# Queries and keys split into rounded and remaining parts before the turn instead of after it

## The reference, cut to what matters

```python
h = concatenate([patch_sums(x) @ channel_weights, txt], axis=1)      # 64 x 228 x 192
xn = norm_scale * layernorm(h) + norm_bias
q, k, v = split(xn @ W_attn + b_attn)                                # 12 heads x 16
q, k = rope(q), rope(k)                                              # rotation by position
att = softmax([sinks, causal(q @ k.T / 4)])[..., 1:]
h = h + ((att @ v) @ W_proj + b_proj) * rezero
h = h + experts(layernorm(h))          # 8 experts, top 2, capacity, gated by silu
```

## Time and profile before

| | us |
|---|---|
| median of 3 executions | 3388.71 (3383.93 to 3389.58) |
| profiled execution, span of its instructions (no other time of it is given) | 3385.4 |
| DVE busy over the span | 2468.5 (73%) |
| PE busy over the span | 3004.5 (89%) |
| POOL busy over the span | 2034.5 (60%) |
| ACT busy over the span | 1363.1 (40%) |

### The profile page before, as it was taken

How to read it: one execution, slowest core, us unless ns; L and a number is a source line. 1 busy time by engine, 2 the same in 40 slices (tenths; PEclk the granted TensorE clock), 3 DMA queues, 4 the chain that set the end, 5 groups by cost and what they waited for, 6 DMA issues and landing times.

```text
span 3385.4 us, 62750 instructions
## 1 busy us (share of the span) xinstructions
PE 3004.5 (89%) x20432; PEld 2601.3 (77%) x20432; DVE 2468.5 (73%) x6258; ACT 1363.1 (40%) x3398; POOL 2034.5 (60%) x1558
## 2 busy tenths in 40 slices
PE   2988889888889888898898898599999999999997
PEld 1777767777777777777777777598989898898987
DVE  3899998999998999989989987354444444444553
ACT  0434444344344344343443444343344443443443
POOL 2666666666666666666666664255555555555655
PEclk9899998999998999989988989799999999999999
DMA  6544544433333333233233320233333333433333
GB/s 190 150 131 138 155 126 138 130 85 102 90 89 103 82 97 103 77 101 99 80 101 89 90 75 23 68 51 62 52 67 49 66 57 56 69 50 65 51 62 48
DMA packets 205961, 297.49 MB, mean 88 GB/s; under 512 B 88374, under 2 KB 167675, under 8 KB 205874
## 3 DMA queue, kind: packets, MB, share of 16 engines
q1 hardware_dynamic: 82994, 243.82, 26.1%
q0 software_dynamic: 122880, 52.55, 11.1%
HBM read 201.73 MB, written 93.90 MB: 87 GB/s over the span
## 4 chain that ended last, share of the span: by engine, by line
issue 31%; POOL 27%; DVE 20%; DMA 12%; PE 7%; POOLq 1%; SPq 1%; ACT 1%; DVEq 0%; ACTq 0%
DMA out<-arena,who 10%; POOL out L1437 8%; POOL moe_rows L1268 6%; POOL qk L721 4%; POOL arena L689 4%; DVE hot L631 3%; DVE place L669 3%; POOL rstd L707 3%; POOL spread L697 3%; DVE arena L1419 2%; DVE pooled L498 2%; DVE pieces L550 2%; PE bank L1409 2%; DVE rot_s L535 1%; DMA prob<-in_w_t 1%
## 5 line engine op out<-in xcount | busy, mean ns | idle before, releaser
L1437 POOL DMA_INDIRECT out<-arena,who x320 | 597.2, 1866 | 202.9 <-issue 198.7
L721 POOL TENSOR_TENSOR qk<-rot_c,rot_s 114x768 f32<-114x768 f32 x256 | 455.2, 1801 | 256.7 <-DVE rot_s L535 253.6
L1395 ACT ACTIVATE arena<-bank 128x456 f32<-128x456 f32 x320 | 175.5, 549 | 634.2 <-PE bank L1386 621.8
L1409 PE MATMUL bank<-prob,arena 128*114 128x192 f32 x2560 | 429.3, 326 | 0.0
L689 POOL TENSOR_TENSOR arena<-arena 112x896 f32<-112x896 f32 x192 | 396.8, 2096 | 44.3 <-DMA arena<-in_x 44.3
L1409 PEld LDWEIGHTS bank<-prob,arena 128*114 128x114 f32 x2560 | 412.2, 178 | 0.0
L1268 POOL DMA_INDIRECT moe_rows<-row,slot x256 | 293.1, 1145 | 185.3 <-issue 185.3
L1401 DVE TENSOR_TENSOR arena<-bank,arena 128x456 f32<-128x456 f32 x320 | 201.7, 630 | 268.5 <-ACT arena L1395 256.6
L571 DVE TENSOR_REDUCE top<-bank 114x2 f32<-114x456 f32 (+1 forms) x576 | 332.0, 622 | 2.5 <-PE bank L903 2.0
L843 PE MATMUL bank<-w_qkv,xn_t 97*114 97x384 f32 x512 | 221.3, 561 | 109.4 <-DVE place L669 108.7
L1426 POOL TENSOR_TENSOR rms<-rms,minus_half 114x4 f32<-114x4 f32 x82 | 85.4, 1042 | 348.0 <-DVE rms L1324 348.0
(11 more groups left out here) (167 smaller groups left out, 7523.2 us busy)
## 6 DMA issues: line engine op xcount, KB each, us to landing
arena<-in_x SPq DMA_DIRECT2D x64, 2352.0 KB, 11.3
arena<-moe_rows SPq DMA_DIRECT2D x82, 363.4 KB
moe_rows<-filler SPq DMA_DIRECT2D x20, 1453.5 KB
out<-h SPq DMA_DIRECT2D x64, 171.0 KB
out<-arena,who POOLq DMA_INDIRECT x320
arena<-in_w_t SPq DMA_DIRECT2D x9, 512.0 KB
arena<-in_w_t SPq DMA_DIRECT2D x18, 256.0 KB
moe_rows<-row,slot POOLq DMA_INDIRECT x256
```

What stands on the lines that cost most here:

```text
L721: nc.gpsimd.tensor_tensor(dst, a, b, ALU.add).then_inc(qk_rotated[t], 1)
L1409: ins = nc.tensor.matmul(bank[6 + s // 2][0:TT, D * (s % 2):D * (s % 2 + 1)], hid[:, j, TT * s:TT * (s + 1)], w_dn[e_par][:, j, :], start= ...
L1437: nc.gpsimd.indirect_dma_start(out=out[:, :], out_offset=bass.IndirectOffsetOnAxis(ap=who[par][:, s:s + 1], axis=0), in_=ys[par][:, s, :], ...
```

## The change

Rounding and subtraction are done while the tokens still lie on the partitions. POOL adds the rotation once, in place in `rot_c` (two instructions of 192 columns for a half). ACT (`high_parts`) then copies the sum into the two rounded places of each head in `qk`, which is now an fp32r tile, in two instructions of 384 columns for a half. POOL (`low_parts`) subtracts what ACT wrote from the sum and writes the two remaining places, again two instructions of 384 columns. The turn becomes a plain matmul with the rounded identity, and what comes out is only copied: a turn of queries by ACT (`place_q`, two instructions), a turn of keys by DVE (`place_k`, one). `round_qk`, `split_qk` and `rounded` are gone.

```diff
-        qk = sb("qk", [TT, 2, 2 * HEADS, 4, HD])
+        qk = sb("qk", [TT, 2, 2 * HEADS, 4, HD], fp32r)
...
         def rotate(dve, at, t):
...
-            wait(dve, qk_rotated[t], 2 * at.b)
+            wait(dve, qk_low[t], at.b)
...
+        def place_q(act, at, r):
+            act.wait_ge(qk_turned[r], at.b + 1)
+            if r == 0:
+                wait(act, scored_t[8], at.b - 1)
...
+                ins = nc.scalar.activation(dst, src[lo, 0:4 * TT].rearrange("p (a n) -> p a n", a=2), ACT.Copy)
+            ins.then_inc(qk_placed[r], 1)
+        def place_k(dve, at, r):
+            dve.wait_ge(qk_turned[r], at.b + 1)
...
+            nc.vector.tensor_copy(dst, src).then_inc(qk_placed[r], 1)
...
         def add_rotation(pool, at, t):
+            pool.wait_ge(qk_read[t], at.b + 1)
             for half in range(2):
-                nc.gpsimd.tensor_tensor(dst, a, b, ALU.add).then_inc(qk_rotated[t], 1)
+                c, sn = (r[:, t, :].rearrange("p (a s k) -> p a s k", s=2, k=8)[:, :, i, :]
+                         for r, i in ((rot_c, half), (rot_s, 1 - half)))
+                ins = nc.gpsimd.tensor_tensor(c, c, sn, ALU.add)
+            ins.then_inc(qk_rotated[t], 1)
+        def low_parts(pool, at, t):
+            pool.wait_ge(qk_high[t], at.b + 1)
+            for hi, lo, of, first in piece_views(t):
+                ins = nc.gpsimd.tensor_tensor(lo, of, first.bitcast(fp32), ALU.subtract)
+            ins.then_inc(qk_low[t], 1)
...
+        def high_parts(act, at, t):
+            act.wait_ge(qk_rotated[t], at.b + 1)
+            wait(act, qk_turned[5], at.b)
+            for hi, lo, of, first in piece_views(t):
+                ins = nc.scalar.activation(hi, of, ACT.Copy)
+            ins.then_inc(qk_high[t], 1)
...
         def turn_qk(pe, at, last, r):
-                pe.wait_ge(qk_rotated[1], 2 * n)
-                pe.wait_ge(qk_rotated[0], 2 * n)
+                pe.wait_ge(qk_low[1], n)
+                pe.wait_ge(qk_low[0], n)
...
-                    ins = nc.tensor.transpose(dst[:, TT * (2 * a + t):TT * (2 * a + t + 1)], src, ident[0:TT, 0:TT])
+                    ins = nc.tensor.matmul(dst[:, TT * (2 * a + t):TT * (2 * a + t + 1)], src, ident_r[0:TT, 0:TT],
+                                           start=True, stop=True)
...
         def step_scalar(act, p, a, m, t, z):
             half1("T5 S7 S8")
+            if a:
+                high_parts(act, a, 0)
             if t:
                 copy_y(act, t)
+            if a:
+                high_parts(act, a, 1)
             if t:
                 copy_yn(act, t)
...
         def step_vector(dve, p, a, m, t, z):
             # split_qk 0, 2, 4 are gone; 1, 3, 5 are place_k at the same places
...
                 if a:
                     add_rotation(pool, a, 0)
+                    low_parts(pool, a, 0)
                 if z:
                     scatter_waits(pool, z, fill)
                 if a:
                     add_rotation(pool, a, 1)
+                    low_parts(pool, a, 1)
```

More of the change, by code:

```diff
@@ L198, in build @@
         rot_s = sb("rot_s", [TT, 2, 2 * D])
-        qk = sb("qk", [TT, 2, 2 * HEADS, 4, HD])
+        qk = sb("qk", [TT, 2, 2 * HEADS, 4, HD], fp32r)
         val = [sb(f"val{i}", [TT + 1, 2, HEADS, 32]) for i in range(2)]
-        rounded = [sb(f"rounded{i}", [128, 4 * TT], fp32r) for i in range(2)]
         pieces = sb("pieces", [128, 16 * HID + 4 * ROWS], fp32r)
@@ L309, in build @@
         qk_rotated = [sem(f"qk_rotated{t}") for t in range(2)]
+        qk_high = [sem(f"qk_high{t}") for t in range(2)]
+        qk_low = [sem(f"qk_low{t}") for t in range(2)]
         qk_turned = [sem(f"qk_turned{k}") for k in range(6)]
-        qk_rounded = sem("qk_rounded")
-        qk_split = [sem(f"qk_split{k}") for k in range(6)]
+        qk_placed = [sem(f"qk_placed{k}") for k in range(6)]
         scored = [sem(f"scored{k}") for k in range(9)]
@@ L536, in rotate @@
                                     sin[:, t, :].unsqueeze(1).to_broadcast([TT, 24, 16]), ALU.mult).then_inc(qk_read[t], 1)
-        def split_qk(dve, at, r):
-            dve.wait_ge(qk_rounded, 6 * at.b + r + 1)
-            src, hi = bank[bank_of("turn", r)], rounded[r % 2]
+        def place_q(act, at, r):
+            act.wait_ge(qk_turned[r], at.b + 1)
+            if r == 0:
+                wait(act, scored_t[8], at.b - 1)
             k = TURNS[r]
-            if r == 0:
-                wait(dve, scored_t[8], at.b - 1)
[L545 to L559, removed]
@@ new lines, in place_q @@
+            src = bank[bank_of("turn", r)]
+            for side in range(2):
+                lo = slice(64 * side, 64 * side + 64)
+                dst = q_t[at.par][lo, :, :].rearrange("p (a s) n -> p a s n", s=2)[:, 2 * k:2 * k + 2, side, :]
+                ins = nc.scalar.activation(dst, src[lo, 0:4 * TT].rearrange("p (a n) -> p a n", a=2), ACT.Copy)
+            ins.then_inc(qk_placed[r], 1)
+        def place_k(dve, at, r):
+            dve.wait_ge(qk_turned[r], at.b + 1)
+            if r == 1:
+                wait(dve, scored_t[8], at.b - 1)
+            kk = TURNS[r] - 3
+            dst = k_t[at.par][:, 2 * kk:2 * kk + 2, :, 0:TT].rearrange("p a t n -> p (a t) n")
+            src = bank[bank_of("turn", r)][:, 0:4 * TT].rearrange("p (a n) -> p a n", a=4)
+            nc.vector.tensor_copy(dst, src).then_inc(qk_placed[r], 1)
@@ L711, in add_rotation, with piece_views @@
         def add_rotation(pool, at, t):
[L712 to L715, removed]
+            pool.wait_ge(qk_read[t], at.b + 1)
             for half in range(2):
[L717 to L720, removed]
-                nc.gpsimd.tensor_tensor(dst, a, b, ALU.add).then_inc(qk_rotated[t], 1)
+                c, sn = (r[:, t, :].rearrange("p (a s k) -> p a s k", s=2, k=8)[:, :, i, :]
[7 more added lines that the diff above has]
+            ins.then_inc(qk_low[t], 1)
+        def piece_views(t):
+            for side in range(2):
+                heads = slice(HEADS * side, HEADS * (side + 1))
+                of = rot_c[:, t, D * side:D * (side + 1)].rearrange("p (a k) -> p a k", k=HD)
+                of, first = (v.unsqueeze(2).to_broadcast([TT, HEADS, 2, HD]) for v in (of, qk[:, t, heads, 0, :]))
+                if side == 0:
+                    parts = qk[:, t, heads, :, :].rearrange("p a (c s) k -> p a s c k", s=2)
+                else:
+                    parts = qk[:, t, heads, :, :].rearrange("p a (s c) k -> p a s c k", s=2)
+                yield parts[:, :, 0, :, :], parts[:, :, 1, :, :], of, first
+        def high_parts(act, at, t):
[4 more added lines that the diff above has]
+            ins.then_inc(qk_high[t], 1)
         def copy_h(act, at):
@@ L764, in copy_v @@
                                  bank[6][0:TT, 0:2 * D].rearrange("p (a k) -> p a k", k=HD), ACT.Copy).then_inc(v_ready, 1)
[L766 to L773, removed]
         def round_shift(act, at):
@@ L866, in bank_free @@
                 if kind == "turn" and m:
-                    return pe.wait_ge(qk_split[k], m.b + 1)
+                    return pe.wait_ge(qk_placed[k], m.b + 1)
                 if kind == "score" and m:
@@ L894, in score @@
             if k < 3:
-                pe.wait_ge(qk_split[2 * k], n)
-                pe.wait_ge(qk_split[2 * k + 1], n)
+                pe.wait_ge(qk_placed[2 * k], n)
+                pe.wait_ge(qk_placed[2 * k + 1], n)
             bank_free(pe, "score", k, at, last)
@@ L1093, in half1 @@
                 for c, k in items.split():
-                    if c == "T" and m:
-                        round_qk(act, m, int(k))
+                    if c == "T" and m and TURNS[int(k)] < 3:
+                        place_q(act, m, int(k))
                     elif c == "S" and t:
@@ L1130, in step_vector @@
         def step_vector(dve, p, a, m, t, z):
-            if m:
-                split_qk(dve, m, 0)
             if t:
@@ L1137, in step_vector @@
             if m:
-                split_qk(dve, m, 1)
+                place_k(dve, m, 1)
             if a:
@@ L1141, in step_vector @@
             if m:
-                split_qk(dve, m, 2)
-            if m:
-                split_qk(dve, m, 3)
+                place_k(dve, m, 3)
             if p:
@@ L1148, in step_vector @@
                 choose(dve, z)
-            if m:
-                split_qk(dve, m, 4)
             if z:
@@ L1157, in step_vector @@
             if m:
-                split_qk(dve, m, 5)
+                place_k(dve, m, 5)
             if p:
```

## The result

The changed kernel takes 3520.7 us (median of 4, 3515.8 to 3528.3) against 3389.1: ratio 1.0394, 95% interval 1.0377 to 1.0410. Forecast were 3485, slower, from 3325 to 3530.

What follows compares the result with a forecast made beforehand. DVE's list was taken to bound pass one at 32.09 us a step. Afterwards a POOL, ACT, PE chain of 31.3 plus 2.4 of clock cost makes 33.7, +96 us on 3388.7: 3485 us, range 3325 to 3530.

Steps and rivals of the forecast that it cites:

- The bound moves from DVE to the chain of hand-overs: Pass one: the chain POOL, ACT, PE sets the step instead of DVE, 31.3 us at full clock against 32.09.
- The pause before `project`: PE has nothing to do from 23.3 to 27.7 us of each step, 4.4 us, as `copy_yn` stands behind `high_parts` 1.
- The clock's price: Half clock on PE's work behind the pause, `project` to `sum_channels`: 2.4 us a step, of between 0 and 3.5.
- Rival 1: PE's pause doesn't bring the clock down, or only under the pause: step 31.3 us, 3341 us in all; chance 0.22.
- The last exponential: On ACT it was to start 15.46 us after `sum_channels`, kept as in the kernel before.
- The turn at nothing: PE's 24 transposes become 24 matmuls of fp32r pieces: priced nothing to 0.6 us a step, nothing taken.
- L669 and those behind it: DVE's stand at L669 and the next instruction, behind POOL's: from up to 1.8 to about 0.5 us each.
- POOL's price by columns: POOL at 2.2 ns a column: 0.52 us for 192 columns (adds), 0.95 for 384 (low parts).
- the gap ahead of the first scatter: On POOL, from low part to first scatter DMA: 0.3 to 1.05 us, 0.6 taken.
- Rival 4: New operations are dearer: 3690 us by POOL's low parts, 3620 by two-record turns, 3515 in milder forms; chance 0.09.
- The range's upper end: 3530 us, from 3.0 us of clock cost a step and the late scatter gap.
- Rival 3: Hand-overs hidden, the step falls with DVE's work until PE bounds it at 29 us: 3203 us; chance 0.04.

Runs made afterwards that it cites:

- e6_before_order: Kernel before, with POOL's list reordered (rotation of half 1 and `spread` ahead of the scatters): 3396.9 us, ratio 1.0028.
- e1_fill: Changed kernel with 17 throw-away matmuls in PE's list ahead of `project`: 3387.3 us, ratio 0.9996.
- e8_fill_transpose: Changed kernel with 17 throw-away matmuls ahead of `project` and the turns as transposes again: 3355.8 us, ratio 0.9911.
- e11_fill_gap: Changed kernel with 17 throw-away matmuls ahead of `project` and `exp_gap` moved behind S5 on ACT: 3358.6 us, ratio 0.9907.
- e2_transpose: Changed kernel with the turns made as transposes again: 3516.6 us, ratio 1.0381.
- e12_order_gap: Changed kernel with scatters last on POOL, turns as transposes, five throw-away matmuls ahead of `turn_xf`, `exp_gap` behind turn 4: 3112.9 us, ratio 0.9186.
- e4_gap: Changed kernel with `exp_gap` moved behind turn 4 and S5 in ACT's list: 3639.6 us, ratio 1.0747.
- e9_before_fill: Kernel before, with eight throw-away matmuls ahead of the second `make_qk`: 3379.7 us, ratio 0.9984.

## Why the prediction was right

The forecast held by its mechanism, not only by its sign: the pause, its cause, the clock behind it and its price came as forecast. Part of the closeness is luck, as errors along the chain cancel. In us from `sum_channels`, for the step shown (1022.88) and as the mean of the 59 steps:

| step | forecast | step shown | mean |
|---|---|---|---|
| last exponential starts | 15.46 | 16.65 | 16.26 |
| low parts 0 done | 18.9 | 20.1 | 19.7 |
| first scatter | 19.5 | 20.3 | 19.9 |
| adds 1 done | 26.0 | 26.9 | 26.5 |
| last score done | 23.3 | 24.6 | 24.2 |
| `project` | 27.7 | 28.4 | 28.0 |
| `project` to the next `sum_channels` | 3.57 + 2.4 | 5.94 | 6.20 |
| step | 33.7 | 34.3 | 34.2 |

- *The bound moves from DVE to the chain of hand-overs*: right. DVE fell to 64% of pass one, and PE's wait for L669 is gone from its list of waits. That DVE set the step before rests on its 92% and on that wait; e6_before_order agrees with it, but doesn't single it out.
- *The pause before `project`, 4.4 us*: 3.8.
- *The clock's price, 2.4 of 0 to 3.5 us*: 2.5 a step between the changed kernel and e1_fill (6.20 and 3.71), and 133 us between the medians, or 2.2 a step.
- *Rival 1*, the clock holds: its condition was wrong, and held by hand its step is 31.6 for 31.3. Its time was 46 us too low, 3341 against 3387, level with before and not faster. e8_fill_transpose and e11_fill_gap show that the form of the turns and the place of `exp_gap` have a part in these 46; how much of them is left when both are mended, no run shows.
- *The last exponential, 15.46*: 0.8 us early, the largest error. Three terms make it. The turns were put at nothing, from L903, and cost 0.2 a step in it (16.26 to 16.04 by e2_transpose). The wait for S5, which the forecast didn't have, costs 0.3 (16.17 in e1_fill, 15.88 in e11_fill_gap). The rest, some 0.3, begins ahead of the second norm, by the timelines: ACT's two copies of turn 2 take 1.09 us where one rounding took 0.55, and PE waits 0.7 to 0.9 for the norm (L1018) where it waited 0.1 to 0.2.
- *The turn at nothing*: the mis-sized term of PE. A turn of four took PE 0.37 us from its start to the next line's before (1038.70 to 1039.07) and 0.50 now (1037.49 to 1037.99), so 0.8 us for six, over the "nothing to 0.6" of the prediction; 0.2 of it reaches the step. L903's 293 ns is a mean over full and half clock. The weight loads of the trace before, which the prediction didn't read, do show the difference, 141 ns for a turn and 178 for pieces (400 to 1900 us), and the new turn's loads take 195:

```profile
L888 PEld LDWEIGHTS bank<-ident,qk 114*128 114x128 f32 x1120 | 116.1, 141 | 30.3 <-issue 24.0 <-POOL qk L721 5.5
L942 PEld LDWEIGHTS bank<-pieces 128*114 128x114 f32 x278 | 49.5, 178 | 4.3
```

- *L669 and those behind it, up to 1.8 us down to 0.5*: 0.50 for L669. But the stand at the fold only moved from L631 to L626 (0.24 to 2.10 us), which is ahead of `exp_gap`: that is where the wait for S5 comes from, and e12_order_gap shows that it was worth 44 us once it lay on the path.
- *POOL's price by columns*: 1005 ns for a low part and 595 for an add, where 950 and 520 were taken; the gap ahead of the first scatter was 0.2 instead of 0.6. The two cancel, and from the last exponential to `project` the chain took 11.7 us instead of 12.2. That takes back much of the 0.8.
- Forecast +96 us, measured +132. The mean step is 0.5 us longer than forecast: 0.8 at the exponential, less 0.5 on the chain, plus 0.2 behind `project`. That is some 30 us over the steps, and what is left of the difference is outside them. *Rival 4* in its milder form (0.5 us a step, 3515) is nearer in number; of its cause, dearer operations, the turns' 0.2 and POOL's 0.3 are there, but the earlier scatters give the latter back.
- *The range's upper end*: 3.0 us of clock cost and the late scatter gap (0.45) on 31.3 would give 34.75 a step and some 3548, not 3530. The 3520.7 lies within either.
- *Rival 3*, 29 us a step once the hand-overs don't matter, was given 0.04 for this order of work. With POOL's order changed, and the clock held, it is what happens: 28.3 and then 27.6 us.

## What to carry to other kernels

When work is taken from the engine that is full, ask which list the new hand-overs stand in and what stands behind them: the relief of 462 us of DVE was worth 1% at most, even with the clock held, until four scatters, which nobody on the path waited for, went to the end of GpSimd's list. In these runs a pause of TensorE of 3.8 us had a second price, 2.2 to 2.5 us of half clock in what followed. Fill such a pause with throw-away matmuls once, to see how large that price is, before small edits are judged: one of them came out with the wrong sign at a falling clock. And read more than one step: here two sorts of steps took turns, and a step of one sort from one kernel held against a step of the other sort from another misleads.

## What the runs showed of the hardware

- An edit's worth can depend on the clock's state: the same move of one small instruction on ACT was -29 us with TensorE kept busy (e11_fill_gap against e1_fill) and +119 us without (e4_gap against the changed kernel).
- At full clock, four plain matmuls of rounded numbers with 128 columns of weights and 114 moving ones take TensorE 0.50 us. As four transposes the same turn takes 0.37 to 0.38, though both show one record for each matmul; weight loads are 195 ns in the changed kernel, and 141 (before) and 149 (e2_transpose) as transposes.
- Pauses of 1.8 us before the change and of 3.8 us after it both bring the granted clock to 0.50 afterwards: the first in 37 stretches over 59 steps, the second in every step. With the pause filled it stays at 1.00 in both (e9_before_fill, e1_fill).
- ACT took 0.54 us for 456 columns on 64 partitions and 0.55 on 115, so splitting a copy by partitions doubled its cost here; before, DVE paid the same way (0.69 on 64 and on 128).
